# The softmax chain on TensorE in a graph-attention kernel: one product for two carries, a transposition that adds, single vectors for the ends, and the differences turned ahead of an expansion

## What is computed

```python
e = leaky_relu(xl[src] + xr[dst], 0.2)             # GATv2; the GAT layer adds two scalars per head
logits = einsum('ehc,hc->eh', e, att)
m = segment_max(logits, dst)                       # maximum over the edges of a node
ex = exp(logits - m[dst])
out = segment_sum(xl[src] * ex / segment_sum(ex, dst)[dst], dst)
```

## Time and profile before

| what | value |
|---|---|
| median of three runs | 4124.04 us |
| profiled execution, its own time | 4115.89 us |
| its span | 4114.1 us |
| mean granted TensorE clock | 0.947 |
| TensorE matmuls, busy | 3659.4 us (89%) |
| TensorE weight loads, busy | 2722.7 us (66%) |
| VectorE / GpSimd / ScalarE, busy | 3149.5 / 2804.3 / 1229.2 us |

### The profile page before, as it was taken

How to read it: one execution, slowest core, us unless ns; L and a number is a source line. 1 busy time by engine, 2 the same in 40 slices (tenths; PEclk the granted TensorE clock), 3 DMA queues, 4 the chain that set the end, 5 groups by cost and what they waited for, 6 DMA issues and landing times. The chain is left out here.

```text
span 4114.1 us, 121899 instructions
## 1 busy us (share of the span) xinstructions
PE 3659.4 (89%) x31817; PEld 2722.7 (66%) x31818; DVE 3149.5 (77%) x8748; ACT 1229.2 (30%) x4200; POOL 2804.3 (68%) x2941
## 2 busy tenths in 40 slices
PE   6699999999999898999999999977788777877875
PEld 5577777777776676777777777745455554555543
DVE  6667877787788665787787787875688788888886
ACT  4433333333333563333333333324111111111113
POOL 5577777777775127777777777723777777777760
PEclk9899999999999999999999999999788889888889
DMA  4354444444443225444444444435545545554544
GB/s 101 107 141 127 132 131 133 127 132 132 132 127 96 62 67 135 131 132 132 127 132 132 131 126 132 126 107 176 136 136 139 137 132 139 139 135 133 139 107 125
DMA packets 333899, 521.05 MB, mean 127 GB/s; under 512 B 152887, under 2 KB 219617, under 8 KB 333809
## 3 DMA queue, kind: packets, MB, share of 16 engines
q0 software_dynamic: 120320, 338.39, 30.1%
q1 hardware_dynamic: 213489, 181.58, 15.4%
HBM read 484.14 MB, written 35.46 MB: 126 GB/s over the span
## 5 line engine op out<-in xcount | busy, mean ns | idle before, releaser
L692 POOL DMA_INDIRECT gathered<-table,idx x2496 | 2610.5, 1046 | 800.1 <-issue 545.9
L1131 PE MATMUL pS<-gathered,Dm 128*128 128x264 f32 x4992 | 1706.2, 425 | 90.6 <-DVE Dm L1537 49.4
L1525 DVE TENSOR_TENSOR acc_mem<-acc_mem,pS 128x264 f32 x2496 | 1041.4, 417 | 133.0 <-PE pS L1131 108.7
L1068 PE MATMUL pZ<-DT,x 128*128 128x128 bf16 x9984 | 1083.7, 221 | 11.8 <-DVE DT L1488 9.0
L1068 PEld LDWEIGHTS pZ<-DT,x 128*128 x9984 | 867.9, 99 | 339.4 <-issue 61.6
L853 ACT ACTIVATE reluT<-pZ 128x256 f32<-128x256 f32 x1664 | 636.9, 383 | 1301.8 <-PE pZ L1074 1182.5
L1074 PE MATMUL pZ<-ident,gathered 128*128 128x128 f32 x3328 | 937.5, 282 | 15.9 <-DMA gathered<-table,idx 15.7
L1131 PEld LDWEIGHTS pS<-gathered,Dm 128*128 128x128 f32 x4992 | 793.0, 200 | 234.1 <-DVE gathered L1554 112.6
L1554 DVE TENSOR_TENSOR gathered<-gathered 128x512 f32<-128x512 f32 x1248 | 852.4, 683 | 65.0 <-ACT gathered L870 64.1
L1537 DVE TENSOR_TENSOR Dm<-iota_row,rel_items 128x256 f32<-128x256 f32 x1248 | 516.5, 414 | 0.0
L1074 PEld LDWEIGHTS pZ<-ident,gathered 128*128 128x128 f32 x3328 | 470.7, 141 | 20.3 <-DMA gathered<-table,idx 18.9
(11 more groups left out here) (230 smaller groups left out, 3372.3 us busy)
## 6 DMA issues: line engine op xcount, KB each, us to landing
DT<-rel_dram SPq DMA_DIRECT2D x156, 512.0 KB
gathered<-table,idx POOLq DMA_INDIRECT x2496
flags<-flag_dram SPq DMA_DIRECT2D x1664, 8.0 KB
span_row<-flag_dram SPq DMA_DIRECT2D x1664, 0.1 KB
table<-xls SPq DMA_DIRECT2D x147, 132.0 KB, 1.9
flags<-flag_dram SPq DMA_DIRECT2D x416, 32.0 KB
gathered<-table SPq DMA_DIRECT2D x98, 132.0 KB, 2.1
gathered<-in_x SPq DMA_DIRECT2D x98, 128.0 KB, 2.1
```

Source lines behind the costliest of these rows:

```text
L692: nc.gpsimd.indirect_dma_start(out=G[:, b, i, :], out_offset=None, in_=tab[l], in_offset=bass.IndirectOffsetOnAxis(ap=idx[:, b, i:i + 1], ...
L1068: mm = nc.tensor.matmul(z_slot(i)[:, half], x3[:, bass.ds(tk[i], 1), s, half].rearrange("p o c -> p (o c)"), moving, start=(s == 0), stop= ...
L1131: nc.tensor.matmul(pS[:, i % 4, 0:ROW], Dm[:, i % 8, :], G[:, at[0], at[1], :], start=True, stop=True).then_inc(seg_done, 1)
L1525: link(v.tensor_tensor(acc_at(n), acc_at(n), pS[:, n % 4, 0:ROW], ALU.add))
```

## The change

It makes four edits in the chain; the work of the other engines is the same but for where the second row of `carry_in` lies.
1. `carry_in` holds its two rows in partitions 0 and 32 of one 128x128 matrix, and one product with two columns of the identity takes the place of two products with one column each.
2. The linear terms are added to the logits by a product flagged as a transposition.
3. Only the first column of `F1` and of `B1` is turned, into partition 0 of `pM`.
4. The two transpositions of `dif` and `mT` at `i == 6`, with their wait for `dif_ready`, stand ahead of `expand(6)` and no longer behind it.

```diff
-        carry_in = sb("carry_in", [P, 2, 8 * GI])
+        carry_in = sb("carry_in", [P, 8 * GI])
...
                         freed = (l < 2 or i % 4 == 0) and (late if i <= GI // 2 else second)
+                        if second and i == 6:
+                            pe.wait_ge(dif_ready, up(dif_ready))
+                            nc.tensor.transpose(pM[:, P:2 * P], dif[:], ident[:])
+                            nc.tensor.transpose(pM[:, 0:P], mT[:], ident[:]).then_inc(dif_turned, 1)
                         if first and l < 2:
                             expand(i, freed)
...
-                            nc.tensor.matmul(pL[:, 0:P], lin[:], ident[:],
+                            nc.tensor.matmul(pL[:, 0:P], lin[:], ident[:], is_transpose=True,
                                              start=False, stop=True).then_inc(logits_done, 1)
...
-                                nc.tensor.transpose(pM[:, 0:P], F1[:], ident[:])
-                                nc.tensor.transpose(pM[:, P:2 * P], B1[:], ident[:]).then_inc(ends_turned, 1)
+                                nc.tensor.transpose(pM[0:1, 0:P], F1[:, 0:1], ident[:])
+                                nc.tensor.transpose(pM[0:1, P:2 * P], B1[:, 0:1], ident[:]).then_inc(ends_turned, 1)
                             if i == 4:
                                 pe.wait_ge(carry_ready, up(carry_ready))
-                                for r in range(2):
-                                    mm = nc.tensor.matmul(pM[:, 256 + r:257 + r], carry_in[:, r, :], ident[:, 0:1], start=True, stop=True)
-                                mm.then_inc(carry_turned, 1)
-                            if i == 6:
-                                pe.wait_ge(dif_ready, up(dif_ready))
-                                nc.tensor.transpose(pM[:, P:2 * P], dif[:], ident[:])
-                                nc.tensor.transpose(pM[:, 0:P], mT[:], ident[:]).then_inc(dif_turned, 1)
+                                nc.tensor.matmul(pM[:, 256:258], carry_in[:], ident[:, 0:33:32], start=True, stop=True).then_inc(carry_turned, 1)
...
-                                    ins = v.tensor_copy(carry_in[0:1, r, :].rearrange("o (h k) -> o h k", h=H), row)
+                                    ins = v.tensor_copy(carry_in[32 * r:32 * r + 1, :].rearrange("o (h k) -> o h k", h=H), row)
```

More of the change, by code:

```diff
@@ L1578, in body @@
                                 if l == 2:
-                                    ins = v.tensor_copy(carry_in[0:1, r, :].rearrange("o (h k) -> o h k", h=H), row)
+                                    ins = v.tensor_copy(carry_in[32 * r:32 * r + 1, :].rearrange("o (h k) -> o h k", h=H), row)
                                 else:
-                                    ins = v.tensor_copy(heads_first(carry_in[0:1, r, :]), in_turns(row))
+                                    ins = v.tensor_copy(heads_first(carry_in[32 * r:32 * r + 1, :]), in_turns(row))
                             ins.then_inc(carry_ready, 1)
```

## The result

The kernel before took 4124.82 us (median of 4 runs, 4122.51 to 4126.01), the changed kernel 4167.58 us (4 runs, 4162.28 to 4169.06). The ratio is 1.0101, 95% interval 1.0088 to 1.0113: 42.8 us slower, where the prediction had 28.5 us. Direction and range held. Part of that is luck: the largest term of its sum is not there, and a larger one that it had at nothing stands in its place. The stages show it first.

The account below looks back on a forecast made before the run. TensorE was taken to bound layers 0 and 1, gathers layer 2. -22.9 - 11.4 + 30.2 + 22.4 + 10.2 = +28.5 us on the profiled 4115.9 gave 4144.4, or 4152 us on the medians' scale; range 4104 to 4178.

Parts of the forecast that it names:

- Carries: TensorE at L1113, layers 0 and 1: two loads fewer, 0.22 us in each of 104 bodies, 22.9 us less.
- Linear terms: TensorE at L1093, layers 0 and 1: one pass instead of two, 0.11 us in each of 104 bodies, 11.4 us less.
- Ends as single vectors: Turns of `F1` and `B1`: one-column operands pay idle time like the scores' 32-column ones, 0.29 us x 104, 30.2 us more.
- the distance at `i == 2`: Sign for the single-vector ends: last L1074 to L1131 about 0.6 us; staying at 0.33 means that edit is misjudged.
- Differences ahead of `expand(6)`: Path from `expand(6)` through `Relu` and exponential to `i == 7` starts 0.22 us later in 102 bodies, 22.4 us more.
- the hold at `i == 7`: Sign for the later path: TensorE's load of L1131 idle 0.55 us, where it was 0.33.
- The just-in-time wait: TensorE's wait for `dif_ready`, now ahead of `expand(6)`: 0.10 us a body, bounds 0 and 0.25, 10.2 us more.
- rival 1: Ends in layers 0 and 1: a one-column operand has no fence, the sum loses 30.2 us, 4122.3 us; chance 0.20.
- Layer 2 at zero: Layer 2: gathers set the pace and no edit touches them, so its time changes by nothing.
- Rival 3: GpSimd paces layers 0 and 1 too: savings worth nothing, costs still count, 4124 us; chance 0.08.
- a fence: Idle time around the scores' 32-column operand, 0.09 + 0.20 us, expected around the one-column ends too: 30.2 us.

Follow-up runs that it names:

- experiment 4: Kernel before, with the ends turned as 32 columns instead of 128: 5245.59 us against 5242.61 on a slower chip, ratio 1.0012.
- experiment 1: One gather in sixteen left out of both kernels: before takes 4051.03 us (ratio 0.9824), the changed kernel 4045.18 us (0.9807).
- experiment 2: Changed kernel with the transpositions of `dif` and `mT` put back behind `expand(6)`: 4103.30 us, ratio 0.9948 to the kernel before.
- experiment 3: Changed kernel with ScalarE's exponential and copy of `i == 6` ahead of the `Relu` of item 6: 4127.06 us, ratio 1.0010 to the kernel before.
- experiment 5: Kernel before, with layer 2's comparison for the one-hot rows reading its row of numbers from PSUM: 5255.52 us against 5242.61 on a slower chip, ratio 1.0022.

## Why the prediction was right, and where it wasn't

Direction and range were right. Of its two savings one came out as said and one larger; of its three costs one is right, one is half as large, and the largest isn't there. That the sum lay near the measured time is luck.

- **Carries, -22.9 us.** Right: 0.47 to 0.24 us, -0.23 a body.
- **Linear terms, -11.4 us.** Right in kind, too small: 0.33 to 0.17, so -0.16 and 16.6 us. My reading, which no run tested: the row that I took had the transposition in a stream, and here it stands behind the scores' pause, with its load and its matmul starting together (918.85).
- **Ends as single vectors, +30.2 us.** Wrong. The step that failed is "the operand is nearer to 32 columns than to 128": the price was taken from the scores because of their width, and width has no price for these transpositions, 0.11 us from start to start with 1 column as with 32 (experiment 4). The lower bound, 0, was the truth, and the sign that the prediction names for a misjudged third edit came: the distance at `i == 2` is 0.34 us (920.93 to 921.27) and not 0.6.
- **Differences ahead of `expand(6)`, +22.4 us.** Right: the path has its 1.65 us again and starts 0.22 us later, and the hold at `i == 7` is 0.55 us in the median, as predicted, where it was 0.33. The growth of VectorE's wait by 52.6 us in all is not this path alone: experiment 1 puts 19.2 us down to it, and the rest is rows that were waited for.
- **The just-in-time wait, +10.2 us.** Too large. The wait came (L1089 0.18 us idle on `dif`), but it costs some 0.05 us in the body shown, for 0.10; one triple behind it takes 0.37 us for 0.33. With the path it makes 0.20 to 0.28 us a body by experiment 2, for 0.32.
- **The sum on TensorE** should thus have been -0.23 - 0.16 + 0.28 = -0.11 us in the short body, and the long one agrees (21.85 to 21.74): -11 us, which is rival 1's account at its lower end. Experiment 1 measures -0.09. The body of 21.41 us that the prediction reads from the earlier trace rows is every second one only; the layers' means are 21.59 and 21.68.
- **Layer 2 at zero: wrong**, +15.0 us. "No edit touches them" is true of the gathers' instructions and false of their duration.
- **Rival 3 named the engine and missed the price.** It worked out 16 x (1.047 + 0.305) = 21.6 us, "as long as a body", and went on to "savings would be worth nothing". It took the 1.047 for a property of the gather. It is 0.946 plus what VectorE adds, and so a term that every edit moves which moves VectorE. The three layers lost 46.8 us where TensorE's own balance is -11 and layer 2 zero: about 58 us, on the scale of the profiled executions, that stand in no line of the sum.

So a forecast of +28.5 for a measured +42.8 was made of a fence that isn't there (30.2) in the place of a lengthening that wasn't seen. What the profile of before would have told: the busy and idle time of GpSimd added up over one layer, and the spread of its gathers, 0.95 to 1.4 us under a mean of 1.05, which asks for a reason.

What isn't settled is why edit 4 brings 264 gathers of layer 0 to start inside a weighing and not 155, and why the first three edits bring 211 of layer 2 to do so and not 177. TensorE, VectorE and GpSimd drive each other there, and the counts differ between kernels with nearly the same order; no row of before would have given them.

## What to carry to other kernels

Take each engine's busy time plus its least pauses over one stage, not over the span: two engines can be full at once, as here 16 x (1.048 + 0.305) = 21.65 us of GpSimd stood beside a body of 21.59, and then a saving on one is met by the other (in experiment 3 TensorE waits 54.3 us for gathered rows, and the time is 24 us behind experiment 2), while a delay of the other costs nearly all of itself (0.38 us a body of longer gathers after the change, of which 0.36 show in layer 0). A mean duration whose single values spread, as the gathers' from 0.946 to 1.45 us here, can be a sum that other engines write into; find out who before you count it as constant. When an instruction is moved ahead of a producer, follow the order of the engine that consumes both: here the exponential starts 0.28 us behind `Relu` with the transpositions behind `expand(6)` (827.99, 828.27) and with them ahead of it (926.83, 927.11), and with the other three edits in, the kernel is 20 us faster or 43 us slower than before by the place of the same two transpositions alone.

## What the runs showed of the hardware

- An indirect gather's issue takes GpSimd 0.946 us where nothing holds it. If it starts inside a weighing that goes on for more than 0.13 us, it ends 0.81 to 0.835 us behind that (478 of 481 before), and so it does inside the comparison (389 of 393 before); it takes up to 1.45 us in all. A weighing that starts behind the gather doesn't hold it (1 of 346); a comparison does only if it starts within 0.07 us (19 of 102 before). The addition of L1525, with an operand in PSUM, doesn't hold it (0 of 891 before), nor does the comparison with one operand in PSUM (0 of 75 in layer 2 of experiment 5; with that operand in SBUF, in experiment 4's kernel, 63 of 78). L1586, with one column in PSUM, does: the 36 gathers over 0.955 us that start inside it end 0.81 to 0.82 us behind it.
- An fp32 transposition with a stationary operand of 1 column (920.93 to 921.27 in the changed kernel) or of 32 (1131.62 to 1131.95 in experiment 4) follows and is followed at 0.11 us, as one of 128 columns.
- Between two gathers GpSimd has 0.303 to 0.306 us in 2457 of the 2495 pauses of before, whichever releaser the rows name; where it waits for a slot it is longer, 0.41 us on the mean in layer 0 of experiment 1 (307.7 over 758).
